# A two-layer graph network on one core: the start reordered, the first attributes fetched early, window preparation moved nearer to its use

## The reference

```python
edge_index = jnp.stack([src, dst])
h = jnp.maximum(_layernorm(x, axis=-1), 0.0)
x = x + _L0_gnn_ref(h, edge_index, W, a)
h = jnp.maximum(_layernorm(x, axis=-1), 0.0)
x = x + _L1_gnn_ref(h, edge_index, edge_attr_128, W_weight, b_weight, W_gate, b_gate)
```

## Time and profile before

| | before |
|---|---|
| median of three runs | 5262.22 us |
| profiled execution | 5246.28 us |
| its span, first to last instruction | 5244.3 us |
| busy: TensorE, VectorE, ScalarE, GpSimd | 4067.9, 3568.8, 2154.4, 3852.1 us |
| first edge loop, first to last gather begun | 112.05 to 2204.15 us |
| second edge loop, first to last scatter begun | 2247.02 to 4377.60 us |

### The profile page before, as it was taken

How to read it: one execution, slowest core, us unless ns; L and a number is a source line. 1 busy time by engine, 2 the same in 40 slices (tenths; PEclk the granted TensorE clock), 3 DMA queues, 4 the chain that set the end, 5 groups by cost and what they waited for, 6 DMA issues and landing times.

```text
span 5244.3 us, 127081 instructions
## 1 busy us (share of the span) xinstructions
PE 4067.9 (78%) x34573; PEld 3194.0 (61%) x34573; DVE 3568.8 (68%) x8411; ACT 2154.4 (41%) x5077; POOL 3852.1 (73%) x4481
## 2 busy tenths in 40 slices
PE   6766666666666666598888888889898985999987
PEld 4455555555555555476666666666666664777665
DVE  7998777777777777754444444444444446999997
ACT  4122222222222222254444444444444444887776
POOL 5777777777777777667777777777777776776776
PEclk9888888888888888899999999999999997999999
DMA  4432222222222222356555555555555557999997
GB/s 146 107 70 70 67 68 67 68 67 67 67 67 67 67 68 67 76 162 176 168 174 174 173 174 168 174 173 173 174 169 174 174 168 239 329 332 323 321 307 233
DMA packets 445970, 801.45 MB, mean 153 GB/s; under 512 B 118726, under 2 KB 276937, under 8 KB 445823
## 3 DMA queue, kind: packets, MB, share of 16 engines
q1 hardware_dynamic: 240978, 426.27, 28.1%
q0 software_dynamic: 143648, 346.93, 22.8%
q10 hardware_dynamic: 61300, 27.75, 1.8%
HBM read 539.83 MB, written 280.79 MB: 156 GB/s over the span
## 4 chain that ended last, share of the span: by engine, by line
POOL 45%; issue 20%; DMA 15%; PE 8%; DVE 5%; ACT 4%; SPq 1%; POOLq 1%; ACTq 1%; DVEq 0%
POOL parts L624 19%; POOL gat L609 13%; POOL rows L609 13%; DMA parts<-rows,sidx 8%; DMA rows<-parts 6%; ACT rows L1149 2%; PE ps L959 2%; PE ps L973 1%; PE ps L757 1%; DVE gat L1786 1%; PE ps L889 1%; PE ps L891 1%; ACT ea L1211 1%; PE ps L979 0%; DVE msg L1575 0%
## 5 line engine op out<-in xcount | busy, mean ns | idle before, releaser
L624 POOL DMA_INDIRECT parts<-rows,sidx x1664 | 1625.0, 977 | 548.5 <-issue 451.1
L799 PE MATMUL ps<-msg,to_node 128*128 128x128 f32 x3328 | 617.3, 362 | 727.3 <-DVE msg L1575 727.3
L889 PE MATMUL ps<-w_edge,gat 128*128 128x256 f32 x3328 | 1068.3, 405 | 0.0
L799 PEld LDWEIGHTS ps<-msg,to_node 128*128 128x128 f32 x3328 | 570.9, 267 | 749.2 <-issue 749.2
L609 POOL DMA_INDIRECT gat<-table,sidx x832 | 790.8, 950 | 258.7 <-issue 258.4
L609 POOL DMA_INDIRECT rows<-table,sidx x832 | 790.3, 950 | 253.4 <-issue 252.8
L1149 ACT ACTIVATE rows<-ps 128x512 f32<-128x512 f32 x832 | 481.1, 607 | 1062.8 <-DMA parts<-rows,sidx 975.7
L891 PE MATMUL ps<-hot,to_edge 128*128 128x256 bf16 x4992 | 863.4, 284 | 0.0
L1107 ACT ACTIVATE earlier<-ps,less_three 128x512 bf16<-128x512 f32 x416 | 263.4, 684 | 1219.2 <-PE ps L808 1212.8
L891 PEld LDWEIGHTS ps<-hot,to_edge 128*128 128x128 bf16 x4992 | 511.5, 102 | 298.7 <-issue 41.5
L889 PEld LDWEIGHTS ps<-w_edge,gat 128*128 128x128 f32 x3328 | 554.3, 203 | 50.8 <-issue 12.2
(11 more groups left out here) (253 smaller groups left out, 8025.5 us busy)
## 6 DMA issues: line engine op xcount, KB each, us to landing
rows<-parts SPq DMA_DIRECT2D x208, 1028.0 KB
ea<-in_edge_attr SPq DMA_DIRECT2D x422, 256.0 KB
parts<-rows,sidx POOLq DMA_INDIRECT x1664
t<-table_a SPq DMA_DIRECT2D x208, 96.0 KB
xt<-table_a SPq DMA_DIRECT2D x208, 96.0 KB
gat<-table,sidx POOLq DMA_INDIRECT x832
rows<-table,sidx POOLq DMA_INDIRECT x832
x1w<-table_a ACTq DMA_DIRECT2D x208, 64.0 KB
```

The source lines that it names most:

```text
L624: nc.gpsimd.indirect_dma_start(out=parts, out_offset=bass.IndirectOffsetOnAxis(ap=sidx[:, s, j:j + 1], axis=0), in_=rows[:, s, j, :], in_o ...
L799: mmi = pe.matmul(out_ps, to_node[:, s % 2, j * P:(j + 1) * P], msg[:, s % 2, j * F:(j + 1) * F], start=(j == 0), stop=(j == J - 1))
L889: pe.matmul(z, eat[:, s % 2, j // 4, (j % 4) * P:(j % 4 + 1) * P], w_edge[:], start=True, stop=False)
```

## The change

At the **beginning**, SP issues the first four loads of x before the edge lists. ScalarE raises the counts first, loads W and `a`, and leaves biases and the other matrices for a second count, `weights_later`; it waits for the constants up to `eps` only. GpSimd makes `eps` and `ident` earlier. TensorE prepares W after `ident` and the first weights; the bias product moves into `limits`, its copy into `group_windows`, and the copies of W into `weights_out`, after the first tile's scaling. The zero stores go ahead of the casts. In `group_limits` the largest id is reduced directly and cut at N - 1 afterwards.

At the **end of the node phase**, a table tile is stored without waiting for its scores, the last scores are counted in `last_scores`, which SP and ScalarE wait for and GpSimd does not, the fill of `ids` covers less, and `next_gather` comes ahead of the keys. In the **histogram** one operation compares two groups, 1024 elements. SP loads the first four groups of **attributes** ahead of the first loop. For the **last group of the first loop** TensorE sums messages first. In the **second loop** SP loads windows four groups ahead, TensorE transposes them two ahead, the split is one ahead, and VectorE's wait for the earlier scatter and the index come ahead of that work; two windows instead of three are prepared before the loop.

```diff
@@ SP
+            for s in range(XU):
+                load_nodes(s, s)
             sp.wait_ge(consts, N_PADS)
...
             sp.wait_ge(nodes_done, 1)
+            sp.wait_ge(last_scores, 16)
...
             for k in range(PIECES):
                 sp.dma_start(piece(x1, k), piece(x, k)).then_inc(x_copied, 16)
...
+            for s in range(U):
+                load_edges(s, s, GE)
...
             for k in range(2):
                 sp.sem_inc(src_st[k], 16)
-            for s in range(U):
-                load_edges(s, s, GE)
...
-                if there(g, 5):
-                    load_window(q + 5, at + 5, (s + 1) % U)
+                if there(g, U):
+                    load_window(q + U, at + U, s)
@@ GpSimd
+            const(nc.gpsimd.memset(eps[:], EPS))
             const(nc.gpsimd.memset(ones[:], 1.0))
+            const(nc.gpsimd.affine_select(out=ident[:], in_=ones[:], pattern=[[-1, P]], compare_op=ALU.is_equal,
+                                          fill=0.0, base=0, channel_multiplier=1))
...
+            def store_table(t, s):
+                pool.wait_ge(node_out, t + 2)
...
+            def store_scores(t, s, stored):
                 pool.wait_ge(scores_up, t + 1)
...
+            store_table(0, 0)
             with pool.Fori(0, T // XU - 1) as i:
                 for s in range(XU):
-                    store_outs(XU * i + s, s)
+                    store_table(XU * i + s + 1, (s + 1) % XU)
+                    store_scores(XU * i + s, s, t_stored[s])
...
-            nc.gpsimd.memset(ids[FULL // 2 // 32 * 32:P], PAD).then_inc(nodes_done, 1)
+            store_scores(T - 1, 0, last_scores)
+            for s in range(XU):
+                pool.wait_ge(t_stored[s], 32 * (tiles_in(s) + 1) - (16 if s == 0 else 0))
+            nc.gpsimd.memset(ids[FULL // 2 // 32 * 32:P, 1, REST:GE], PAD).then_inc(nodes_done, 1)
@@ TensorE
-            pe.wait_ge(consts, N_CONST)
-            pe.wait_ge(weights, N_WEIGHT)
+            pe.wait_ge(consts, N_IDENT)
+            pe.wait_ge(weights, N_FIRST)
...
+                pe.wait_ge(weights_later, N_LATER)
+                pe.matmul(ps[:, 7, 0:2 * F], ones[0:1, :], bias_row[:], start=True, stop=True)
                 pe.wait_ge(once_up, 1)
...
                 pe.wait_ge(digits_up, q)
+                sum_messages(U - 1, q - 1).then_inc(last_ps, 1)
                 turn_keys(U - 1, q - 1)
-                sum_messages(U - 1, q - 1)
                 pe.wait_ge(picked_up, q)
+                pe.wait_ge(copied0, q + 2)
...
-                if there(g, 3):
-                    turn_window((s + 3) % U, q + 3, 2 * turn + (s + 1) // 2)
+                if there(g, 2):
+                    turn_window((s + 2) % U, q + 2, 2 * turn + (s + 1) // 2)
@@ ScalarE
+            act.sem_inc(node_xn, XU)
             act.dma_start(w0[:], W).then_inc(weights, 16)
...
-            act.wait_ge(consts, N_CONST)
+            act.wait_ge(consts, N_EPS)
...
             act.wait_ge(nodes_done, 1)
+            act.wait_ge(last_scores, 16)
@@ VectorE
-                    link(nc.vector.scalar_tensor_tensor(prep_tmp[0:n], e, float(N), e, ALU.is_lt, ALU.mult))
-                    link(nc.vector.tensor_reduce(ends[0:n, 2 + k:3 + k], prep_tmp[0:n], AX.X, ALU.max))
+                    link(nc.vector.tensor_reduce(ends[0:n, 2 + k:3 + k], e, AX.X, ALU.max))
+                link(nc.vector.tensor_scalar(ends[:, 2:4], ends[:, 2:4], float(N - 1), None, ALU.min))
...
+                link(nc.vector.tensor_copy(bias[:], ps[:, 7, 0:2 * F]))
...
                 ids_of_gathers()
+                for s in range(V):
+                    next_gather(s, s)
                 key_of(0)
...
-                    hot_r[:, s, 0:4:2], iota_b[:, 0:2], key[:, bass.ds(g, 1), :, :].rearrange(
-                        "p g d j -> p (g d) j").unsqueeze(2).to_broadcast([P, 2, B, J]), ALU.is_equal)
+                    hot_2[:, 4 * s:4 * s + 4, 0], iota_b[:, 0:1].to_broadcast([P, 4, B, J]), key[:, bass.ds(g, 2), :, :].rearrange(
+                        "p g d j -> p (g d) j").unsqueeze(2).to_broadcast([P, 4, B, J]), ALU.is_equal)
...
-                dve.wait_ge(last_ps, 2 * w + 1)
+                dve.wait_ge(last_ps, 3 * w + 1)
+                add_sums(q - 1)
+                dve.wait_ge(last_ps, 3 * w + 2)
                 pick(U - 2, q - 2, G - 2)
-                add_sums(q - 1)
...
                 nc.vector.tensor_tensor(shift[:], shift[:], inside[:], ALU.mult).then_inc(dve1, 1)
-                if there(g, 2):
-                    dve.wait_ge(part_dve, 2 * q + 12)
-                    first_rest((s + 2) % U, q + 2)
-                dve.wait_ge(spread_up[1], f + 2)
-                dve.wait_ge(z1_up, 4 * U + 4 * q)
-                by_node(to_edge_h[(s + 1) % 2]).then_inc(to_edge_up[1], 1)
...
                 dve.wait_ge(placed[s], 16 * J * turn + 32)
...
                 nc.vector.tensor_tensor(sidx[:, s, :], shift[:], dump[:], ALU.add).then_inc(sidx_up, 1)
+                if there(g, 1):
+                    dve.wait_ge(part_dve, 2 * q + 10)
+                    first_rest((s + 1) % U, q + 1)
+                dve.wait_ge(spread_up[1], f + 2)
+                dve.wait_ge(z1_up, 4 * U + 4 * q)
+                by_node(to_edge_h[(s + 1) % 2]).then_inc(to_edge_up[1], 1)
+                if there(g, 1):
+                    third_part((s + 1) % U, q + 1)
+                if there(g, 2):
+                    window_bias((s + 2) % U, q + 2)
+                if there(g, 3):
+                    window_scale((s + 3) % U, q + 3)
```

More of the change, by code:

```diff
@@ L398, in load_edges @@
                     sp.sem_inc(ea_in[s], 16)
+            for s in range(U):
+                load_edges(s, s, GE)
+            passes = sp.value_load(passes_i[0:1, 0, 2:3], min_val=1, max_val=WINDOWS)
+            with sp.Fori(0, passes) as w:
+                sp.wait_ge(pass_go[0], w + 1)
+                sp.sem_inc(past_waits, 1)
+                with sp.Fori(0, GU) as i:
+                    for s in range(U):
+                        sp.wait_ge(expanded, U * (w * GU + i) + s + 1)
+                        sp.sem_inc(past_waits, 1)
+                        first = window_start(U * i + s)
+                        sp.dma_start(sdw[:, s, :], score_dst[bass.ds(first, P), :]).then_inc(sdw_in[s], 16)
+                sp.sem_inc(pass_done[0], 1)
+            sp.wait_ge(pass_done[0], 2 * passes + 1)
+            sp.sem_inc(past_waits, 1)
             for k in range(2):
                 sp.sem_inc(src_st[k], 16)
-            for s in range(U):
-                load_edges(s, s, GE)
             def load_window(n, g, s):
@@ L558, in _ @@
             assert step[0] == N_CONST, step[0]
+            for s in range(XU):
+                at = N + P // XU * s
+                for table, empty, done in ((score_dst, zeros[:].bitcast(BF16)[0:P // XU, 0:3 * HEADS], t_stored),
+                                           (table_a, zeros[0:P // XU, :], t_stored)):
+                    pool.dma_start(table[at:at + P // XU, 0:empty.shape[1]], empty).then_inc(done[s], 16)
             pool.wait_ge(edges_in, 96 * len(CH))
@@ L564, in _ @@
                                           prep_int(k)[:, s, :].rearrange("g (p j) -> g p j", j=J)).then_inc(real_up, 1)
-            for s in range(XU):
-                at = N + P // XU * s
-                for table, empty, done in ((score_dst, zeros[:].bitcast(BF16)[0:P // XU, 0:3 * HEADS], t_stored),
-                                           (table_a, zeros[0:P // XU, :], t_stored)):
-                    pool.dma_start(table[at:at + P // XU, 0:empty.shape[1]], empty).then_inc(done[s], 16)
             pool.dma_start(x1[N:N + P, :], zeros[:, 0:F]).then_inc(tails, 16)
@@ L924, in _ @@
                     turn_half(0, w * G, w * GU, h)
-                for g in range(3):
+                for g in range(2):
                     turn_window(g, w * G + g, 2 * w * GU)
@@ L1179, in _ @@
                     evict_turned(0, w * G, h)
-                for g in range(U):
+                for g in range(2):
                     window_root(g, w * G + g)
-                source_root(0, 2 * w * GU)
                 window_out(w * G)
@@ L1186, in _ @@
                 second_part(0, w * G)
[L1187 to L1190 removed]
+                for g in range(2, U):
+                    window_root(g, w * G + g)
+                source_root(0, 2 * w * GU)
                 with act.Fori(0, GU - 2) as i:
@@ L1490, in _ @@
             nodes()
-            for s in range(V):
-                next_gather(s, s)
             key_of(1)
```

174 lines of the change are left out of this document (77 added, 97 removed).

## The result

The changed kernel takes 5266.4 us (median of 20 runs), the kernel before 5251.89 us beside it: ratio 1.0025, 95% interval 1.0018 to 1.0033. It is slower by 0.25% by the ratio and by 14.5 us by the medians, where 21 us less were forecast; 5266.4 us lies above the stated range of 5224 to 5260 us.

| us | before | after | difference |
|---|---|---|---|
| first comparison of the histogram | 108.43 | 110.74 | +2.3 |
| first to last comparison | 70.57 | 79.99 | +9.4 |
| 65th gather begun | 203.22 | 215.05 | +11.8 |
| 65th gather to end of the last | 2001.9 | 2001.8 | -0.1 |
| idle before the first scatter | 41.93 | 37.80 | -4.1 |

A forecast was written before the change was run, and what follows sets the result against it. GpSimd's gather and scatter issues were taken to bound both loops, DMA the third. 16 us up to the 65th gather plus 5 between the loops gave 21 us, so 5241 us by the median, range 5224 to 5260.

The forecast's parts named there:

- The beginning: Start of the kernel: with x sent first, the first reciprocal at 10.75 us; 7.2 us gained, bounds 3 and 9.
- Two edits hide behind that: Start: zero stores ahead of casts, and a_diag loads ahead of bias loads, cost nothing; the stores 4 us if uncovered.
- Limits: Group limits after the fourth node tile: less VectorE work, VectorE being the engine waited for; 1.9 us gained.
- End of the node phase: Before the first gather: table store earlier, landing awaited by others, smaller memset; 3.7 us gained, for GpSimd alone.
- Histogram: Up to the 65th gather: comparisons take 63 us, 7.6 less; gather at 187.2 us, 16 us gained including earlier steps.
- nothing saved in the histogram: Lower bound of the gain up to the 65th gather, if double width doubles a comparison's cost: 12 us.
- Attributes: SP's queue ahead of the first loop: four attribute loads delay the first scores; 2 us charged, from 0 to 14.
- rival 1: Attributes hold up the first scores: 65th gather at 201 us, gain 7 us, 5255 us; chance 0.17.
- Between the loops: From last gather to first scatter: later last add offset by SP's emptied queue and shorter window preparation; 5 us gained.
- Second loop: Scatter loop: no change, as GpSimd has three prepared groups in front and a group still takes 10.25 us.
- rival 3: Second loop becomes TensorE's, 0.2 us a group: 42 us lost there, net 21 slower, 5283 us; chance 0.09.
- 10.25 us a group: Second loop: sign that the forecast holds, GpSimd's scatters of a group of eight taking as long as before.

The follow-up runs named there:

- e11: Kernel before with only GpSimd's eight zero stores moved ahead of its four casts; one run, first gather at 116.21 instead of 112.05 us.
- e2: Changed kernel with GpSimd's four casts ahead of its eight zero stores again; ratio to before 1.0013 (1.0004 to 1.0022).
- e1: Changed kernel with the histogram comparing one group of 512 elements at a time again, four ahead of TensorE; ratio to before 1.0006 (0.9994 to 1.0017).
- e4: Changed kernel with the wide comparisons four groups ahead of TensorE instead of two; ratio to before 0.9994 (0.9984 to 1.0005).
- e10: Changed kernel with the first edge attributes loaded after the first loop again; one run, idle before the first scatter 41.91 us against 37.80.
- e8: Changed kernel with e4, e2 and e5 together; ratio to before 0.9994 (0.9983 to 1.0005).
- e9: Changed kernel with e4, e2, e5 and e7 together; ratio to before 0.9991 (0.9981 to 1.0001).
- e12: As e9, but with the four casts on ScalarE and the zero stores first; ratio to before 0.9991 (0.9982 to 1.0000).
- e5: Changed kernel with the last group's key products ahead of the sum of its messages again; ratio to before 1.0040 (1.0027 to 1.0054).
- e6: Changed kernel with both window-splitting subtractions of the second loop replaced by one-operand reductions, leaving the splitting out; ratio to before 0.9994 (0.9985 to 1.0003).
- e7: Changed kernel with VectorE's wait for the earlier scatter and the index at the end of the step again; ratio to before 1.0017 (1.0006 to 1.0028).
- e3: Changed kernel with every edit of the second loop and its beginning undone; ratio to before 1.0015 (1.0004 to 1.0025).

## Why the prediction was wrong

Up to the 65th gather, VectorE freed the first slot at 212.91 us where 184.6 were forecast. Of these 28.3 us, some 11.4 arose ahead of the first comparison (2.3 us lost, 7.2 + 1.9 forecast as gain) and 17.0 in the histogram (9.4 lost, 7.6 forecast as gain).

**Bounds.** Right: GpSimd's issues set both loops. The inference "no step of the change alters the number of issues or one issue" failed: the earlier trace rows give a mean of 977 ns, not how it is made up. Issues of 0.97 us and some of up to 1.23 lay in it, and the timeline of the second loop would have shown them.

**The beginning (7.2 us forecast; 2.3 lost by the first comparison).** The reciprocal came at 11.54 us (10.75 forecast): ScalarE's last weight issue ended at 9.82 us, not at the 9.1 of the sum, whose 0.3 us for the counts no row gave. Two steps behind it failed. The first was the landing of a_diag, "4.19 us after their issue": they landed 9.4 us after the last issue, and the copies of w0t came at 15.40 us. No run shows why; x and the edge lists now share the time, and in the other traces with these loads the copies came between 12.6 and 16.0 us, so part of it is chance. The second was "Two edits hide behind that": the zero stores were priced by who waits for the casts; what the casts keep waiting while they run was left out. In after it was 6.6 us (6.75 for an operation of 0.16), in e11 about 4. With the casts first, as in e2, some 5.3 us of it stay: x's early loads bring VectorE's operations into the casts in either order. The rule was at hand on the page that the prediction quoted for the histogram: the Trainium skill, "SBUF — State Buffer", section "Who interferes with whom", says that a VectorE instruction with two SBUF inputs contends with a GpSimd instruction that reads SBUF. By that the trace agrees: 6.75 us for 4 columns beside the casts. It also names tensor_scalar among the operations that can contend, if their operands meet conditions, and the 3.95 us for two of them in e2 agree.

**Limits (1.9 us).** The failed step is "VectorE is the engine waited for there". It was by 0.4 us only. The work went as forecast (2.3 us less, and a bias copy of 0.42 later), but then ScalarE's copies of the ids ended last, 1.2 us after VectorE, and TensorE's bias product came behind them. In all twelve traces with this edit the copies end last, by 1.2 to 2.0 us, and at the eighth reciprocal nothing of the gain is left. No run undoes this edit alone; the account rests on these rows.

**End of the node phase (3.7 us).** Right: the first gather against the first comparison, 3.62 to 0.16 us, 3.5.

**Histogram (16 us, with the steps ahead of it).** The failed step is "0.605 us for each of the 104 ... 63 us". The cost of an operation was near (0.65 in pairs). What was left out is the distance between VectorE and TensorE: two buffers of double width instead of four make the two engines take turns, 1.52 us for four groups instead of 1.36. The bound "nothing saved in the histogram" excluded a loss, with no row for it. e1 and e4 show it: the 65th gather comes 8 to 12 us earlier without the turns. The rule that the prediction quotes there from the Trainium skill forecast slower gathers, and they were (1.21 us); but e4 has them at 0.94 beside operations of the same width, so width was not the cause, and what ties gathers to that cycle is not settled.

**Attributes (2 us, rival 1).** Nothing was lost, by e10, but because the histogram was later than the scores. With an early histogram, as the forecast assumed, the first window of scores is awaited 4.6 to 5.7 us (e4, e8, e9, e12), some 3 to 4 more than in after; rival 1 is not out for that case.

**Between the loops (5 us).** Right, by its parts too: 4.1. The store of the last sums came 5.0 us later, counted from the last gather's end (5.2 forecast; e5 gives 6.1 us for the order of products); from there to the first window's load were 6.89 us (6.8 forecast, 8.14 before), and it landed within 1.8 (2.2 forecast, 5.86 before). So the first window landed as long after the last gather as before, as forecast, and from landing to scatter it took 3.8 us less (5.2 forecast). These are single executions; with the same order here, the idle time ranges from 36.2 to 38.0 us.

**Second loop (0).** Neither the forecast nor rival 3: TensorE did not hold anyone up, and the idle time stayed "issue". The step that failed is the mean again: the second loop was priced by who waits for whom, and an issue was taken as fixed. The wait ahead of the splitting made two VectorE operations begin more often just ahead of an issue of GpSimd: 8.6 us in one execution, shown by e6 and e7. The sign "10.25 us a group" was too coarse to see 0.04 us.

## What to carry to other kernels

Before an instruction run of GpSimd is moved, list the VectorE operations with two SBUF operands in its new place: each may wait until the run ends. Before the time saved on one engine is counted, look at which other engine's work ends at the same wait: here 0.4 us behind. When an operation in a ring of buffers is made twice as wide, keep the number of buffers; half as many turn an overlap into taking turns. Where an issue of one engine sets a loop, look at how its mean is made up before its price is called fixed.

## What the runs showed of the hardware

- Four casts on GpSimd kept a VectorE operation waiting for 6.75 us (after) and 4.86 us (e11), to the end of the run and not of one cast; in e2 operations got in between two casts, in parts of 0.68, 3.95 and 1.62 us. In e1, e3, e4, e5 and e6 the held operation began 0.8 to 1.2 us ahead of the first cast, beside the last zero stores, and lasted 8.0 to 8.5 us; in e5 and e6 it was a tensor_scalar of 128 columns.
- An indirect DMA issue of GpSimd grew from 0.97 to as much as 1.23 us when a VectorE subtraction with two SBUF operands had begun just ahead of it (106 of 131 in after), not when the subtraction began while the issue ran (none of 281), and not with a reduction of the same 0.42 us (none of 115 in e6).
- Gathers took 1.04 us beside narrow comparisons, 1.21 beside wide ones two ahead and 0.94 beside wide ones four ahead. No run settles why.
- A cast of 1024 columns from int32 took 1.78 us on ScalarE (e12) and 1.8 on GpSimd.
